# A state-space layer in fp32: softplus as one ScalarE instruction, and dt and dt*u stored and restored without the bf16 split

## The reference

```python
x_dbl = jnp.einsum('bkdl,kcd->bkcl', xs, x_proj_w)
dts, Bs, Cs = jnp.split(x_dbl, [R, R + N], axis=2)
dts = jnp.einsum('bkrl,kdr->bkdl', dts, dt_projs_w)
dts = jax.nn.softplus(dts + dt_projs_b[None, :, :, None])
As = -jnp.exp(A_logs).reshape(K, DI, N)
def step(h, inp):
    u_t, d_t, B_t, C_t = inp
    dA = jnp.exp(d_t[..., None] * As)
    h = h * dA + (d_t * u_t)[..., None] * B_t[:, :, None, :]
    y = jnp.einsum('bkcn,bkn->bkc', h, C_t)
    return (h, y)
```

## Time and profile before

| | |
|---|---|
| executions | 4308.70, 4313.52, 4328.05 us |
| span of the profiled execution | 4322.2 us |
| TensorE busy | 3375.4 us (78%) |
| VectorE busy | 3524.7 us (82%) |
| ScalarE busy | 2718.5 us (63%) |
| GpSimd busy | 1598.8 us (37%) |
| mean granted TensorE clock | 0.858 of full speed |

### The profile page before, as it was taken

How to read it: one execution, slowest core, us unless ns; L and a number is a source line. 1 busy time by engine, 2 the same in 40 slices (tenths; PEclk the granted TensorE clock), 3 DMA queues, 4 the chain that set the end, 5 groups by cost and what they waited for, 6 DMA issues and landing times. The chain is left out here.

```text
span 4322.2 us, 110119 instructions
## 1 busy us (share of the span) xinstructions
PE 3375.4 (78%) x46784; PEld 1688.2 (39%) x46784; DVE 3524.7 (82%) x3560; ACT 2718.5 (63%) x4416; POOL 1598.8 (37%) x1151
## 2 busy tenths in 40 slices
PE   6788873157777776317777778868999999999998
PEld 4476631012222223101222222553566566666553
DVE  5555476989999967789999996759988888888882
ACT  2365628845555544865555543534899999999995
POOL 0122220079999961009999995000000000000000
PEclk9799986568888887657888877977999999999999
DMA  5334203433232210353223321451221212222211
GB/s 130 83 67 75 54 18 91 145 79 79 71 76 71 66 49 10 112 146 74 72 65 77 76 61 39 126 153 41 56 56 56 64 56 56 64 56 56 56 41 49
DMA packets 160560, 309.95 MB, mean 72 GB/s; under 512 B 69592, under 2 KB 105752, under 8 KB 156101
## 3 DMA queue, kind: packets, MB, share of 16 engines
q1 hardware_dynamic: 159124, 301.24, 27.0%
q10 hardware_dynamic: 944, 1.67, 0.2%
HBM read 194.44 MB, written 107.83 MB: 70 GB/s over the span
## 5 line engine op out<-in xcount | busy, mean ns | idle before, releaser
L2323 DVE TENSOR_REDUCE l3a_mx<-l3a_mx 128x2 f32<-128x768 f32 x1296 | 1165.1, 952 | 160.2 <-PE l3a_mx L2222 156.1
L2289 ACT ACTIVATE l3a_p<-l3a_s 128x384 f32<-128x384 f32 x2592 | 1181.5, 492 | 113.2 <-PE l3a_s L2236 105.7
L1545 POOL TENSOR_TENSOR l_scan_sc<-l_scan_s,l_scan_repc 128x768 f32<-128x768 f32 x576 | 1032.3, 1837 | 5.9 <-DVE l_scan_s L1523 5.7
L1487 ACT ACTIVATE l_scan_da<-l_scan_da,l_k_a 128x768 f32<-128x768 f32 x576 | 503.9, 875 | 627.7 <-PE l_scan_da L1407 627.6
L2236 PE MATMUL l3a_s<-l3a_q,l3a_k 125*32 125x384 f16 x10368 | 802.1, 327 | 5.8 <-DMA l3a_q<-l3a_m 3.9
L2222 PE MATMUL l3a_mx<-l3a_k,l3a_q 124*32 124x384 f16 x10368 | 672.0, 334 | 57.4 <-DMA l3a_q<-l_qx 30.4
L1407 PE MATMUL l_scan_dup<-l_scan_du,l_k_pick 96*128 96x512 bf16 (+1 forms) x1152 | 347.2, 390 | 317.6 <-DMA l_scan_dt<-l_dtp 159.1
L2248 PE MATMUL l3a_o<-l3a_p,l3a_vh 128*32 128x288 f32 x6912 | 568.7, 405 | 0.8 <-issue 0.5
L1536 POOL TENSOR_TENSOR l_scan_bup<-l_scan_dus,l_scan_repb 128x768 f32<-128x768 f32 x192 | 352.6, 1837 | 484.6 <-DMA l_scan_repc<-l_bcp 484.6
L2190 POOL TENSOR_TENSOR l3a_norm<-l3a_out,l3a_spread 128x576 f32<-128x576 f32 x24 | 34.5, 1437 | 1342.1 <-DMA l3a_spread<-l_inverses 1342.1
L1407 PE MATMUL l_scan_da<-l_scan_dt,l_k_pick 96*128 96x512 bf16 (+1 forms) x1152 | 340.6, 384 | 156.1 <-DVE l_scan_s L1523 152.6
(11 more groups left out here) (215 smaller groups left out, 4295.3 us busy)
## 6 DMA issues: line engine op xcount, KB each, us to landing
l3a_q<-l_qx SPq DMA_DIRECT2D x96, 486.0 KB
l_scan_du<-l_dup SPq DMA_DIRECT2D x144, 144.0 KB
l_scan_dt<-l_dtp SPq DMA_DIRECT2D x138, 144.0 KB
l_scan_repb<-l_bcp SPq DMA_DIRECT2D x48, 384.0 KB
l_scan_repc<-l_bcp SPq DMA_DIRECT2D x46, 384.0 KB
l_dtp<-l_prep_high_t SPq DMA_DIRECT2D x16, 432.0 KB, 3.1
l_dup<-l_prep_high_u SPq DMA_DIRECT2D x16, 432.0 KB, 3.1
l_dtp<-l_prep_middle_t SPq DMA_DIRECT2D x16, 432.0 KB, 3.1
```

Of the source, the lines that this page charges most:

```text
L1487: act.activation(da_ps[st % 2][:, 0:TC], da_ps[st % 2][:, 0:TC], ACT.Exp, scale=A[:, column:column + 1]).then_inc(exped, 1)
L1545: pool.tensor_tensor(SC[:, st % NSC, :], S[:, n, :], REPC[k % 2][:], ALU.mult).then_inc(weighted, 1)
L2289: act.activation(P[:, k % NP, third * SW:(third + 1) * SW], s_ps[u % NS_PS][:, 0:SW], ACT.Exp)\
L2323: dve.tensor_reduce(MX[:, qt % (NB * KT), 2 * pair:2 * pair + 2], mx_ps[n % NR][:, :, 0:RG], AX_X, ALU.max)\
```

## The change

In the preparation one Softplus activation per piece reads PSUM, adds the bias and writes dt in fp32; a second activation, Copy, moves the 32 rows of B and C out of the same PSUM piece. VectorE takes the maximum with `DT_LEAST` and multiplies by u. Unit by unit three stores go out: B and C, dt, dt*u, the last two in fp32. The bf16 parts, their buffers and their waits are gone.

In the scan one tile `DTU` of 128 partitions holds, for a chunk, dt of the first 384 positions on partitions 0 to 31, dt of the second 384 on 32 to 63, and dt*u in the same manner on 64 to 95 and 96 to 127. A restore is two fp32 matmuls of 32 rows, 128 columns of weights and 384 positions. They use different groups of 32 rows of the array, and write columns 128 to 511 and 512 to 895 of the PSUM tile (`MID`), so each has a bank of its own. `PICK` is fp32 with its pattern on four row groups.

```diff
-                    act.activation(E[:], X[0:DI, n % 2, :], ACT.Abs).then_inc(absed, 1)
-                    act.wait_ge(absed, n + 1)
-                    act.activation(E[:], E[:], ACT.Exp, scale=-1.0).then_inc(exped, 1)
...
-                    act.activation(LN[:], Wb[:], ACT.Ln).then_inc(logged, 1)
...
-                        act.activation(high[w][:, n % 2, :], whole(w, n), ACT.Copy).then_inc(highed[w], 1)
...
-                        act.activation(middle[w][:], whole(w, n), ACT.Copy).then_inc(middled[w], 1)
...
+                    if n >= 2:
+                        for x in (bc_stored, dt_stored):
+                            act.wait_ge(x[i], 16 * (n // 2))
+                        act.wait_ge(du_done, n - 1)
                     for j, (at, w) in enumerate(WIDE):
                         m = n * NW + j
                         act.wait_ge(made, m + 1)
...
+                        act.activation(dt, bank[0:DI], ACT.Softplus, bias=bias[:, k:k + 1]).then_inc(taken, 1)
+                        act.activation(bc, bank[DI:128], ACT.Copy).then_inc(taken, 1)
...
+                for n in range(UNITS):
+                    i = n % 2
+                    dt = T[0:DI, i, :]
+                    dve.wait_ge(taken, (n + 1) * NW * 2)
+
+                    dve.tensor_scalar(dt, dt, DT_LEAST, None, ALU.max).then_inc(floored, 1)
+                    dve.wait_ge(floored, n + 1)
                     if n >= 2:
...
+                        dve.wait_ge(du_stored[i], 16 * (n // 2))
+                    dve.tensor_tensor(D[:, i, :], dt, source(n), ALU.mult).then_inc(du_done, 1)
...
-        self.PICK = s.sb("pick", [DI, 4, 128], BF16)
+        self.PICK = s.sb("pick", [128, 4, 128])
...
+    HALF = TC // 2
+    MID = slice(CH - HALF, CH + HALF)
...
-        DT = [s.sb(f"dt{i}", [DI, NT, TC], BF16) for i in range(2)]
-        DU = [s.sb(f"du{i}", [DI, NT, TC], BF16) for i in range(2)]
+        DTU = [s.sb(f"dtu{i}", [128, NT, HALF]) for i in range(2)]
...
-                    for dst, src in ((DU, du_dram), (DT, dt_dram)):
-                        for part in range(3):
-                            sp.dma_start(dst[i][32 * part:32 * part + 32, :, :],
-                                         src[p, part, :, span(c)].rearrange("(t e) l -> e t l", t=NT))\
+                    for row, src in ((64, du_dram), (0, dt_dram)):
+                        for h in range(2):
+                            sp.dma_start(DTU[i][row + 32 * h:row + 32 * h + 32, :, :], halves(src, p, c, h))\
                               .then_inc(loaded[i], 16)
...
-                    for at, w in BANKS:
-                        mm = pe.matmul(out[:, at:at + w], PICK[:, g, :], src[k % 2][:, tl, at:at + w],
+                    for h in range(2):
+                        rows = slice(row + 32 * h, row + 32 * h + 32)
+                        at = MID.start + h * HALF
+                        mm = pe.matmul(out[:, at:at + HALF], PICK[rows, g, :], DTU[k % 2][rows, tl, :],
                                        start=True, stop=True)
                     mm.then_inc(done, 1)
```

More of the change, by code:

```diff
@@ L1008, in ssm_prepare @@
         wdt = s.sb("wdt", [DT_R, ND, DI])
[L1009 removed]
+        bias = s.sb("bias", [DI, ND])
         weights = s.sb("weights", [DI, ND, 128])
[L1011 to L1013 removed]
+        T = s.sb("t", [128, 2, L])
         D = s.sb("d", [DI, 2, L])
[L1015 to L1019, removed]
         x_ps = [s.ps(f"x{i}", [128, 2, CH]) for i in range(NP)]
@@ L1022, in ssm_prepare @@
             s.sem(n) for n in ("loaded", "folded", "placed", "made", "taken"))
[L1023 to L1031, removed]
+        floored, du_done = s.sem("floored"), s.sem("du_done")
+        bc_stored, dt_stored, du_stored = (
+            [s.sem(f"{n}{i}") for i in range(2)] for n in ("bc_stored", "dt_stored", "du_stored"))
         def unit(n):
@@ L1219 @@
+                dve.wait_ge(du_done, UNITS)
 class LateConstants:
@@ L1330, in span, with halves @@
             return slice(c * TC, (c + 1) * TC)
+        def halves(dram, p, c, h):
+            at = c * TC + h * HALF
+            return dram[p, :, at:at + HALF].rearrange("(t e) l -> e t l", t=NT)
         def way(ap, d):
@@ L1348, in load_first @@
                 def load_first():
-                    for part in range(3):
-                        sp.dma_start(DU[0][32 * part:32 * part + 32, :, :],
-                                     du_dram[0, part, :, span(0)].rearrange("(t e) l -> e t l", t=NT))\
+                    for h in range(2):
+                        sp.dma_start(DTU[0][64 + 32 * h:96 + 32 * h, :, :], halves(du_dram, 0, 0, h))\
                           .then_inc(loaded[0], 16)
@@ L1402, in _, with restore @@
             def _(pe):
-                def restore(st, src, out, done):
+                def restore(st, row, out, done):
                     k, p, d, c, n = place(st)
                     g, tl = divmod(n, NT)
-                    for at, w in BANKS:
-                        mm = pe.matmul(out[:, at:at + w], PICK[:, g, :], src[k % 2][:, tl, at:at + w],
+                    for h in range(2):
+                        rows = slice(row + 32 * h, row + 32 * h + 32)
+                        at = MID.start + h * HALF
+                        mm = pe.matmul(out[:, at:at + HALF], PICK[rows, g, :], DTU[k % 2][rows, tl, :],
                                        start=True, stop=True)
@@ L1456, in _ @@
             def _(act):
-                for part in range(3):
-                    act.dma_start(DT[0][32 * part:32 * part + 32, :, :],
-                                  dt_dram[0, part, :, span(0)].rearrange("(t e) l -> e t l", t=NT))\
-                       .then_inc(loaded[0], 16)
+                for h in range(2):
+                    act.dma_start(DTU[0][32 * h:32 * h + 32, :, :], halves(dt_dram, 0, 0, h)).then_inc(loaded[0], 16)
                 act.dma_start(REPC[0][:], bc_dram[1, :, span(0)].unsqueeze(0).to_broadcast([8, NS, TC]))\
@@ L2477, in shape_constants @@
 def shape_constants():
-    bf16 = mybir.dt.np(BF16)
     k = {}
```

153 lines of the change are left out of this document (30 added, 123 removed).

## The result

The changed kernel takes 4209.0 us, the median of four executions (4189.11 to 4226.89), beside 4317.34 us for the kernel before on the same chip: ratio 0.9748, 95% interval 0.9712 to 0.9785. It is faster, inside the range of 4030 to 4290 us, and 104 us above the 4105 us that I gave. The profiled execution is the slowest of the four, 4226.89 us with a span of 4225.1 us; the others had a mean granted clock of 0.875 to 0.885, this one 0.872. Of the executions further down, one of e7 (4155.57 us, clock 0.899) and one of e12 (4603.91 us, clock 0.729) were much slower than the others of their kernel; the ratios leave them out.

What follows compares the result with a forecast made beforehand. VectorE was taken to bound the preparation, GpSimd the scan. 4328.05 - 252 (preparation) - 4 (loads) + 48 (half clock) = 4120 us for the profiled execution; median 4313.5 - 208 = 4105 us, range 4030 to 4290.

Steps and rivals of the forecast that it cites:

- The preparation: Preparation of both layers: 63 us instead of 189.5 each, units at 6.5 us near the stores; 252 us saved, 234 to 276.
- What would show it: Signs listed beforehand: preparation 60 to 65 us, DMA share near 0.9, restore matmuls starting together, mean clock over 0.9.
- The loads: Between preparation and scan: 8 loads instead of 12 for the first two chunks, 4 us saved in both layers, 0 to 8.
- The restore: Scan, TensorE: two fp32 matmuls on different row groups run side by side, 0.65 us a restore, 2.03 us a step.
- rival B: Scan restores: row groups run one after the other, 3.33 us a step, TensorE the bound, 4610 us; chance 0.14.
- fp32 weight loads: Scan restores: 128-column loads take 273 ns instead of 101, costed at nothing because they run beside the half before.
- The clock: Scan: a tenth at half clock, where a step takes 3.7 us; 48 us lost for both layers, 0 to 166.
- The evidence against: A stretch from 2855 to 2974 us, 0.50 throughout with TensorE busy 75.48 us, named against the clock rising.
- Rival A: Scan: pairs side by side but not keeping up; clock as low as now, 4223 us, or halves delayed, 4230; chance 0.22.
- Rival C: Preparation doesn't shrink as said: Softplus dearer than Exp or stores queueing, 15 us or more a unit, 4240 us; chance 0.04.
- The forecast's 4105: Whole kernel: predicted median after the change, 4105 us, from a median before of 4313.5 less 208; chance 0.60.
- The sum's start: Start of the sum: 4328.05 us, taken for the profiled execution, with the median before 14.5 us below it.

Runs made afterwards that it cites:

- e7: e3 with one restore step in three on 32 rows, dt and dt*u side by side as in the changed kernel: 4111.4 us, ratio 0.9518.
- e12: e7 with ScalarE's copy of dt*u put ahead of the copy of y at a chunk's end: 4082.7 us, ratio 0.9439.
- e11: The changed kernel with only ScalarE's order changed, copy of dt*u ahead of the copy of y: 4084.4 us, ratio 0.9455.
- e3: The changed kernel with each fp32 restore matmul spanning 64 rows, a selection with zeros picking dt or dt*u: 4124.6 us, ratio 0.9538.
- e6: The changed kernel with both halves of a restore on the same group of 32 rows: 5253.2 us, ratio 1.217.
- e5: The kernel of two bf16 parts (4238.5 us) with restores over 128 rows instead of 64, the added rows zeros: 4119.7 us, ratio 0.9546.

## Why the prediction was right or wrong

- **The preparation, 252 us saved (234 to 276)**: right, 238, near the lower end (2 x 118 and 2 x 137 are 236 and 274, where I wrote 234 and 276). A unit was to be bound by its stores at 6.5 us and took 6.7 and 7.2 in the mean; Softplus cost what Exp does, as assumed; VectorE was busy 31.3 us as said. In layer 1 it was 10.4 us to the first store (8.7 expected), 47.1 for seven units (45.5) and 11.4 for the end (8.9). The DMA share was 0.76, not 0.9: the queue isn't filled without gaps, and 240 GB/s is less than the 298 I worked with. "What would show it" named 60 to 65 us; it was 69 and 72.
- **The loads, -4 us (0 to 8)**: in its range, -1.7.
- **The restore, 0.65 us, two turns**: the mechanism was right, rival B was wrong, and the row that decided it (the column groups) was the right one to lean on. I missed an overlap that helps: dt and dt*u also use different row groups, so a step at half clock is 2.94 us and not 3.7.
- **fp32 weight loads, costed at nothing**: not quite. The halves of a restore follow each other at 0.42 us (1101.57 to 1101.99) instead of 0.32, and at half clock at 0.80 (1121.28 to 1122.08) instead of 0.64. At the full clock this stays well under the pace; at half clock TensorE is the bound, so there it counts. That it is the weight load that shows isn't shown, and I have not priced it apart. The Trainium skill (TensorE: Matmul & The Clock Gate, Part 2) gives fast weight load to 128-column weights that aren't fp32; the trace agrees, with 221 ns in the mean for a load of `PICK` in fp32 against 101 in bf16.
- **The clock, "I take a tenth of the scan at half clock", +48 us (0 to 166)**: this is the step that failed. The scans lost 154 us. I had reasoned from TensorE's busy share, because busy stretches of before ran at the full clock. The runs showed two other things in its place. First, the rows that matmuls span: in the bf16 scan 64 rows gave 0.50 throughout, 128 rows with zeros 0.96, at the same instructions. The gate, which I took as the near case, has matmuls on 96 rows, my restores have 32; I compared busy shares and didn't compare the shapes. Second, the end step: ScalarE's order made a step of 3.1 us with the bf16 restores, 0.42 us from dt*u to the sum, and one of 3.9 us with the fp32 ones; each of the 36 falls of the clock began there or one step on, and with the order changed (e11) only 11% of the scan was left at half clock. I left the boundary between chunks out altogether: no row of mine showed one.
- **The evidence against, 2855 to 2974 us at 0.50**: I named it and gave it little weight. It isn't a case of few rows either: its matmuls have 96 and 124 rows, and TensorE is busy 75 of 119 us.
- **Rival A, the clock stays as low as now: 4223 us**, chance 0.22: its first form is what happened (38% of the scan at half clock instead of 33, 4209 us), and my range holds the result because it was drawn wide enough for this rival. That its number comes so near is luck: a step at half clock costs 0.6 us rather than 1.3, but more of the scan is at half clock and the end steps add 35 us. **Rival B**: its condition didn't occur; where I made the halves follow each other it cost 5253 us, more than the 4610, since the clock fell as well. **Rival C**: no.
- **The forecast's 4105** is near e11's 4084, where the clock is 0.95 and the scans lose 11 us over before; I had put 48.
- **The sum's start, 4328.05**: in every run with both on record the execution lies 1.8 us above its span (4226.89 and 4225.1), so the profiled one before was hardly that of 4328.05 us, 5.85 above. Nothing hangs on it, since the sum takes the 14.5 us out again.

What stays open: how rows and the pause at the chunk's end act together. Either remedy alone lifts the clock from 0.81 to 0.94 or more (e3, e11), so neither is the sole cause, and I haven't tried the pause by itself in a kernel of 128 rows at other lengths. Nor do the rows of one matmul put the kernels in order: fp32 restores on 32 rows, side by side, ran at 0.81 and 0.95, bf16 restores on 64 rows at 0.50. In e3 and e6 the overlap of dt and dt*u, or of the two halves, changed along with the rows in use; only e5 changed rows alone, and e11 the order alone. Nor is it explained why the untouched code took 9.5 us more before the first preparation and, behind the last copies of y, 5.5 us less.

## What to carry to other kernels

When a change makes matmuls use fewer rows of the array, don't judge the clock by TensorE's busy share: look up the granted clock of stretches whose matmuls have the same shape, and try the layout with more rows, even if they hold zeros. After a change, look at the steps that break the rhythm (here each twelfth) and at which step the clock falls; an engine that does the postponable copy before the awaited one can cost more through the clock than by its own length (here some 87 us against 57). And price the two halves of a change apart: here dropping the split was worth nothing as the change stood, and 124 us with the scan mended (4208.5 against 4084.4 us; the new order was not tried with the split kept).

## What the hardware showed that I hadn't expected

- Zeros count: rows 64 to 127 held nothing but zeros, and the scan's clock went from 0.50 to 0.96.
- A TensorE that is nearly always busy can stay at half clock: 738 us (711 of them busy) in the kernel with two parts, 1260 us (1258 busy) with both halves on one row group.
- Four fp32 matmuls on four row groups, from two restores issued 0.27 us apart, took 1.1 us together at the full clock, though the program issues them pair by pair.
- One Softplus of 96 x 1024 out of PSUM takes 1.11 us, and it shares a table with Copy: one table load of 1.28 us in the preparation of layer 1 instead of fifteen.
